# A graph layer kernel: the edge table walked by source block, convolution sums kept in PSUM, and the table zeroed in one stream at the start

## What is computed

```python
# layer 0: five steps of a normalised sum over neighbours
w = dinv[row] * dinv[col]                        # with self loops
for _ in range(5):
    m = segment_sum(w[:, None] * h[row], col)
    h = 0.2 * m + 0.8 * x
x = layernorm(x + h)

# layer 1: gated convolution over the edges
gate = silu(edge_attr @ W1.T + b1) @ W2.T + b2                 # (E, 48)
gate = gate + sum(emb[z[src]] * (emb[z[dst]] @ adaptW.T), -1)  # one number per edge
cw   = where(dist < 6, 0.5 * (cos(pi * dist / 6) + 1), 0)
mj   = node_vec[dst]
agg  = segment_sum(gate * h[dst] * (cw * mj)[:, None], src)
tot  = segment_sum(mj, src)
y    = layernorm_affine(h + agg / clip(tot, 1e-8))
x    = layernorm(x + y)
```

## Time and profile before

| | us |
|---|---|
| three executions timed | 6258.89, 6261.76 (median), 6287.83 |
| profiled execution, its span | 6194.9 |
| index_edges | 105.9 |
| adjacency | 2122.3 |
| propagate | 2249.0 |
| chunks of convolve | 1516.9 |
| busy: PE, DVE, POOL, ACT | 4476.3, 3441.7, 2956.9, 2078.0 |
| slot_table zeroed, SP | 52 DMAs of 1249.5 KB |

### The profile page before, as it was taken

How to read it: one execution, slowest core, us unless ns; L and a number is a source line. 1 busy time by engine, 2 the same in 40 slices (tenths; PEclk the granted TensorE clock), 3 DMA queues, 4 the chain that set the end, 5 groups by cost and what they waited for, 6 DMA issues and landing times. The chain is left out here.

```text
span 6194.9 us, 143286 instructions
## 1 busy us (share of the span) xinstructions
PE 4476.3 (72%) x50445; PEld 3376.9 (55%) x50445; DVE 3441.7 (56%) x8812; ACT 2078.0 (34%) x3637; POOL 2956.9 (48%) x2872
## 2 busy tenths in 40 slices
PE   0477667757776758777777877777758888888885
PEld 0234333333333436556555656565548878787885
DVE  2366666666656553233233323332358888888888
ACT  0133333333333321111111111111126666666664
POOL 1454444544445433433433343334327767676765
PEclk9976777677667577787777877877868888888887
DMA  4222222222222235555555555555401111111111
GB/s 90 63 96 95 95 93 98 90 79 84 95 95 95 85 148 207 182 193 205 201 186 195 214 185 196 206 203 186 172 17 52 42 46 44 44 44 44 44 44 26
DMA packets 292648, 710.09 MB, mean 115 GB/s; under 512 B 203212, under 2 KB 232972, under 8 KB 240894
## 3 DMA queue, kind: packets, MB, share of 16 engines
q1 hardware_dynamic: 226190, 577.45, 27.2%
q10 hardware_dynamic: 7488, 80.35, 3.1%
q0 software_dynamic: 58672, 47.56, 2.7%
HBM read 514.57 MB, written 195.39 MB: 115 GB/s over the span
## 5 line engine op out<-in xcount | busy, mean ns | idle before, releaser
L486 POOL DMA_INDIRECT slot_table<-w_pay,w_slot x1750 | 1802.3, 1030 | 2493.7 <-DVEq L651 1931.0
L927 PE MATMUL pL<-p_parts,p_adj 128*128 128x144 bf16 x12250 | 1093.6, 251 | 498.7 <-issue 440.6
L927 PEld LDWEIGHTS pL<-p_parts,p_adj 128*128 128x128 bf16 x12250 | 950.8, 110 | 644.3 <-issue 607.4
L567 ACT ACTIVATE w_hid<-w_pH,b1c 48x512 f32<-48x512 f32 (+1 forms) x450 | 301.8, 671 | 1927.3 <-DMA cw_table<-cw 976.4
L798 PE MATMUL pA<-ohk,ohb 128*128 128x392 bf16 x2400 | 645.8, 421 | 252.1 <-DVE ohk L769 99.5
L647 DVE COPY w_pay<-w_meta 128x24 f32<-128x24 f32 (+1 forms) x250 | 45.5, 182 | 1363.9 <-PE w_pG L534 1024.0
L534 PE MATMUL w_pG<-w2T,w_hid 49*128 49x48 f32 x3500 | 574.6, 310 | 94.1 <-ACT w_hid L567 56.4
L534 PEld LDWEIGHTS w_pG<-w2T,w_hid 49*128 49x128 f32 x3500 | 515.2, 221 | 224.1 <-issue 205.4
L769 DVE TENSOR_SCALAR ohk<-io_k,k 128x392 bf16<-128x392 f16 x2400 | 621.9, 327 | 7.4 <-issue 7.4
L1300 PE MATMUL cG<-c_cur,c_ohdT 128*128 128x81 bf16 x7350 | 552.0, 212 | 67.4 <-issue 64.4
L1302 PE MATMUL cG<-c_emb,c_ohsT 128*128 128x32 bf16 x7350 | 534.4, 183 | 78.6 <-issue 78.6
(11 more groups left out here) (229 smaller groups left out, 6139.9 us busy)
## 6 DMA issues: line engine op xcount, KB each, us to landing
p_adj<-adj_table SPq DMA_DIRECT2D x250, 1568.0 KB
adj_table<-adj ACTq DMA_DIRECT2D x50, 1568.0 KB
slot_table<-zero SPq DMA_DIRECT2D x52, 1249.5 KB
c_rows<-slot_table SPq DMA_DIRECT2D x50, 1249.5 KB, 5.4
w_attr<-in_edge_attr_dram SPq DMA_DIRECT2D x50, 700.0 KB
slot_table<-w_pay,w_slot POOLq DMA_INDIRECT x1750
kw<-key_table SPq DMA_DIRECT2D x800, 1.5 KB
out_dram<-h_all SPq DMA_DIRECT2D x1, 1152.0 KB
```

What stands on the lines that cost most here:

```text
L486: pool.indirect_dma_start(slotT, bass.IndirectOffsetOnAxis(ap=slot[:, t:t + 1], axis=0), pay[:, t, :], None, bounds_check=SLOTS - 1, oob_i ...
L927: x_ = nc.tensor.matmul(pL[:, half, o * H3:(o + 1) * H3], adj[:, q, n * P:(n + 1) * P], parts[:, n, :, :].rearrange("p t f -> p (t f)"), s ...
```

## The change

The slot table is laid out by source block: a slot's address was (D, r, S) and is now (S, r, D), so `slots_of` takes a source block, `pos` is built from a new per-window tile `home` = S * 128 * 49 + inv, and the base of a destination block grows by 1 instead of 49 * 128. `convolve` walks source blocks outside and destinations inside, 49 x 7 = 343 chunks. All chunks of one source block add into the same 147 columns of PSUM, so the sums stay there for seven chunks, and DVE takes them out once (`take_sums`). One matmul of 147 columns per bucket covers the three parts of its messages. The parts are no longer bf16 tiles: the moving operand is the upper 16-bit half of each fp32 word, read in place with a step of two, and POOL makes the second and third words by two subtractions one after the other (`lower_parts`), without ACT. `tabp` (destination features) is read by PE directly, and the small `cur` holds the source block's embedding. The first body of 14 chunks now stands ahead of the loop, the loop runs 23 times, and seven chunks stand behind it. The clears at the start of `convolve` are gone except that of `c_gx`. The whole slot table (49 regions) is zeroed by ACT at the start of `index_edges`, ahead of Sin on that engine; POOL waits once for all of it before its first scatter; SP no longer zeroes, and `s_clear` is gone.

```diff
-        slots_of = lambda D: slotT.rearrange("(d r s) w -> r d (s w)", r=P, s=NB)[:, bass.ds(D, 1), :]
+        slots_of = lambda S: slotT.rearrange("(s r d) w -> r s (d w)", r=P, d=NB)[:, bass.ds(S, 1), :]
...
             @block.scalar
             def _(act):
+                if beside:
+                    beside(act)
                 act.wait_ge(s_arg, 1)
                 nc.scalar.activation(cw[:, :], cw[:, :], ACT.Sin, bias=halfpi[0:SP_, :], scale=-pi / CUTOFF).then_inc(s_sin, 1)
...
+                    def zero_slots(act):
+                        act.wait_ge(s_z, 1)
+                        for S in range(NB):
+                            act.dma_start(slots_of(S), zero[:, :].unsqueeze(1)).then_inc(s_zero, 16)
+                    cut = cutoff("icut", block, ew, cw, zero_slots)
...
-                        for D in range(2):
-                            sp.dma_start(slots_of(D), zero[:, :].unsqueeze(1)).then_inc(s_zd, 16)
...
-                        sp.wait_ge(s_zd, 16 * 2)
...
+                        nc.vector.memset(zero[:, :], 0.0).then_inc(s_z, 1)
                         nc.vector.memset(bad[:, :], 0.0)
-                        nc.vector.memset(zero[:, :], 0.0).then_inc(s_z, 1)
...
+                nc.vector.scalar_tensor_tensor(home[:, :], f_i[:, 0, :], float(P * NB), inv[:, :], ALU.mult, ALU.add)
...
-                            for n in range(2):
-                                sp.dma_start(slots_of(2 * it + 2 + n), zero[:, :].unsqueeze(1)).then_inc(s_zd, 16)
...
+                        pool.wait_ge(s_zero, 16 * NB)
                         with pool.Fori(0, ND // 2) as it:
-                            pool.wait_ge(s_clear, it + 1)
                             win.scatter(pool, it)
...
+                msg = sb("c_msg", [P, 4, 3, CH * W1c], F32, c)
+                upper = msg[:, :, :, :].rearrange("p q t f -> p (q t f)").bitcast(BF16).rearrange(
+                    "p (q t j w e) -> p q t j w e", q=4, t=3, j=CH, e=2)[:, :, :, :, :, 1]
...
+                        def lower_parts(k, i):
+
+                            q = RING[k % NCK]
+                            pool.wait_ge(s_msg, i + 1)
+                            nc.gpsimd.tensor_tensor(part(k, 1), part(k, 0), upper[:, q, 0, :, :], ALU.subtract).then_inc(s_r1, 1)
+                            pool.wait_ge(s_r1, i + 1)
+                            nc.gpsimd.tensor_tensor(part(k, 2), part(k, 1), upper[:, q, 1, :, :], ALU.subtract).then_inc(s_r2, 1)
...
-                        nc.vector.memset(tabp[:, ND - 1, :, :], 0.0)
-                        nc.vector.memset(agg[:, :, :], 0.0)
-                        nc.vector.memset(gx[:, :, :], 1.0)
...
+                        nc.vector.memset(gx[:, :, :, :], 1.0)
...
-                            nc.vector.tensor_tensor(A, A, pO[:, par, 0:CH * W1c].rearrange("p (s w) -> p s w", w=W1c), ALU.add).then_inc(s_agg, 1)
...
+                            dve.wait_ge(s_O, S * NCK + NCK)
+                            nc.vector.tensor_reduce(agg[:, bass.ds(S, 1), :].rearrange("p o w -> p (o w)"),
+                                                    pO[:, u, 0:W3].rearrange("p (t w) -> p w t", w=W1c), AX, ALU.add).then_inc(s_agg, 1)
...
-                            nc.scalar.activation(mp[:, (k - 1) % 2, 0, :, :], msg[:, (k - 1) % 2, :, :], ACT.Copy).then_inc(s_p0, 1)
...
-                            nc.scalar.activation(mp[:, (k - 1) % 2, 1, :, :], msg[:, (k - 1) % 2, :, :], ACT.Copy).then_inc(s_p1, 1)
...
                             for j in range(CH):
-                                for t in range(3):
-                                    m = nc.tensor.matmul(pO[:, k % 2, j * W1c:(j + 1) * W1c], ohs[:, (k - 2) % NCK, :, j], mp[:, k % 2, t, j, :],
-                                                         start=t == 0, stop=t == 2)
+                                m = nc.tensor.matmul(pO[:, u, 0:W3], ohs[:, ck, :, j], upper[:, RING[ck], :, j, :],
+                                                     start=ck == 0 and j == 0, stop=ck == NCK - 1 and j == CH - 1)
```

184 lines of the change are left out of this document (81 added, 103 removed).

## The result

| | us | ratio to the kernel before |
|---|---|---|
| before, timed beside it | 6272.15 (4 runs) | |
| changed kernel | 6336.81 (6327.26 to 6347.6) | 1.010 [1.007, 1.0131] |
| forecast | 6285, 6195 to 6372 | |

The change made the kernel 1.0% slower, 64.7 us where +23 was forecast.

A forecast was written before the change was run, and what follows sets the result against it. Index_edges was taken as bound by round trips, adjacency by POOL waiting for DVE, convolve by DVE without gaps; +128 - 15 - 90 gave +23 on 6261.8, so 6285 us, range 6195 to 6372.

The forecast's parts named there:

- rival C: Convolve: strided 16-bit reads leave no gain per chunk; convolve -35 us, total 6340; chance 0.18.
- Rival B: Index_edges: ACT's issues aren't held or loads keep their share; +45 to +60 us, total 6212, faster; chance 0.22.
- The stream: Index_edges: zeroing 62.7 million bytes at 398 GB/s lasts 157 us, starting near 25 us.
- Who waits for it: Index_edges: ACT is held by its zeroing issues, Sin runs at about 178 us, and the stage grows by 128 us.
- rival D: Index_edges: `first_i` starved by packet turns, landing at 182 us, Sin at 211; stage +150 us, total 6307; chance 0.20.
- A: The forecast itself, with ACT held in index_edges until some 7 regions are left; own range 6240 to 6330 us; chance 0.40.
- Adjacency: Adjacency without zeroing on SP gains 0.6 us in each of 25 iterations: -15 us, bounds -60 and +25.
- A chunk: Convolve: an undisturbed chunk falls from 3.61 to 3.47 us, the larger of two computed limits; bounds 3.25 and 3.75.
- the round of POOL and DVE: Convolve: POOL and DVE exclude each other, so their operations in turn limit a chunk to 3.47 us.
- the loop through PE: Convolve: the dependency loop through the sums spans two chunks and limits one to 3.40 us, or 3.64 at half speed.
- Convolve in all: Convolve: shorter chunks 48, seven fewer 25, one turn fewer 7, less 5, prologue clears 5: -90 us.
- The base: Whole kernel: the median lies 66.9 us above the profiled span of 6194.9, taken to stay the same around it.

The follow-up runs named there:

- e6: The kernel before, unchanged, profiled on chip 2 in one set with e5b; span 6171.6 us.
- e5b: The changed kernel, unchanged, profiled again on chip 2 in one set with e6; span 6217.6 us.
- e5: The changed kernel, unchanged, run again on chip 3; 4872.37 us, ratio 1.0052 to the kernel before on that chip.
- e8: The changed kernel with ACT starting the zeroing only once `first_i` has landed; index_edges took 221.3 us against 241.9 in the changed kernel on that chip.
- e10: The changed kernel with one of the seven sum matmuls per chunk of convolve; chunks took 1190.5 us together against 1401.3 in the changed kernel.
- e2: The kernel before with only the zeroing moved: all 50 regions by ACT ahead of Sin; 6302.22 us, ratio 1.021 to the kernel before.
- e7: The changed kernel with the old slot numbers and without `home`; adjacency took 1641.9 us against 1631.2 in e5.
- e4b: The changed kernel with the sums reading a contiguous bf16 table, not every second half-word; convolve's chunks took 1397.1 us against 1404.5 in e5.
- e11: The changed kernel with 24 regions zeroed behind Sin, 25 at adjacency's start, and convolve's loop written out; 4623.26 us, ratio 0.9539 to the kernel before.

## Why the prediction was near, step by step

The time fell in the range, 52 us above the predicted 6285, and slower was the likelier side. As a change it is less near: +23 was forecast, and the sets have +64.7 (the first), +46 (the pair e6 and e5b) and +23.1 (e5, chip 3). That the sum of the stages came out close was in part luck. In the pair, index_edges (+8.5) and adjacency (+33) lay above the forecast, propagate, held at 0, took +11.8, and convolve with its prologue lay 29 below. The time is also next to rival C's 6340 and outside the forecast's own 6240 to 6330, but C said that a chunk gains nothing, and it gained 0.225 us. What made the +65 of the first set larger than the +46 of the pair isn't known. Rival B (0.22) fell with index_edges: it had +45 to +60. By the sign that the prediction set itself, no stage held unchanged moved by more than 30 us: propagate with norm0 has +26.8 in the first profiles and +11.8 in the pair.

- **The stream** (step: 157 us at 398 GB/s from 25). Right: the DMA engines moved 408 GB/s from 25.70 to 146.72, and from 180 on ACT's queue moved less than 0.1 MB.
- **Who waits for it** (step: ACT is held, Sin at 178, index_edges +128). The size was near, +136.5, but the mechanism that set it was rival D, to which I gave 0.20: `first_i` at 179.40 (182 worked out), Sin at 207.32 (211). The working of D had one number wrong: SP's queue had moved 9167 packets, most of `first_i`, by 28.8, so that some 430 elements per DMA engine were unread and not 750. That is still as many as the stream had packets per engine (392 rows and the small ones that end each DMA), and so `first_i` came in with the stream's end; with half as many unread it would have come half way through, by the same taking of turns (an estimate from the 935 against 935). D's own sum for the stage was +150: Sin came 4 us sooner than it had it, and what follows Sin was 7 us shorter than before, since the two zeroings are gone from its end. ACT was held as in A, but only to 146.7: at 0.41 MB per us some 39 regions had been written by then, so about ten stood in its queue and not seven. e8 shows that both mechanisms exist one behind the other.
- **Adjacency** (step: -15). The gain isn't there: +18 in the pair, which is within what two like profiles differ by (29, e5b and e10), and e2, with no iteration shorter, shows that nothing was to be won: the zeroing rode beside work with nothing behind it, as the earlier trace rows said. The 0.6 us per iteration had no row. What makes the changed kernel's adjacency longer on the slower chips isn't settled.
- **A chunk** (step: 3.47 from the round of POOL and DVE; the loop through PE 3.40). The loop was right to 0.02 (3.385) and was the binding one. The round was mis-sized: 3.24 (e10) where I added 3.47. e10's chunk from 4926.35 to 4929.60 has, against the terms of my sum: `c_ohd` and `c_gx` 1.30 (1.30), what of `c_ohs` lies behind `c_gx` 0.54 (0.58), what of L1109 lies behind `c_ohs` 0.62 (0.70), the gap 0.08 (0.05), L1111 0.76 (0.79), and `c_ohd` starts 0.05 before L1111 ends (0.05 behind it). No single term was far out; all but the gap were a little too long. S was 0.55 for 0.48: 147 columns and not 144, and 9 ns each for the step; the rest of the loop was 0.10 shorter than worked out.
- **Convolve in all** (step: -90). It was -119 with the prologue (-112.0 - 7.1). Undisturbed chunks gave more, 342 x (3.61 - 3.385) = 77 for my 48. The turn of the loop saved (7) gave nothing: 23 turns cost 174 us before (23 chunks of 257.2 us where 83 are due) and 22 cost 177 in the changed kernel.
- **The base.** I treated the 66.9 us between the profiled span and the median as time around the span. It is 4 to 5 us. The sum was added to the median as a difference, so the forecast didn't suffer; the sum on the span, 6218, would have been 62 us further off.
- **What I passed over.** The 7.48 us at each turn of the loop was in my hands, and I took it as given ("one turn fewer, 7"). It was the largest item in convolve: 22 turns, 177 us. The profile's line for q8, 280 packets in the kernel before, is the row that would have told it.

## What to carry to other kernels

A transfer of many small elements starved here when another queue was given large rows, since the two queues took turns by packets and not by bytes, and everything that waited for it came behind the whole stream: look at what is in flight when a long stream starts, and not only at what its own issuer does next. When a loop's turn shows an idle time that no data explains, look at the instruction queue, and count the instructions of the longest engine's body; writing the loop out can be worth more than the change one set out to make. Compare stages only between profiles from one set of runs, and profile the same kernel twice there before reading a difference of 1%.

## What the runs showed of the hardware

The chips differ, and only in some stages. The changed kernel on chip 3 (e5), propagate with norm0:

```profile
1895.86:3363.97 1468.11, 1375.71 (x15498) 1134.81 (x15498) 768.35 (x1957) 337.34 (x530) 950.74 (x875) 0.96 0.83 300
```

and on chip 2 (e5b):

```profile
2398.73:4713.10 2314.37, 1750.86 (x15498) 1344.44 (x15498) 757.05 (x1957) 338.75 (x530) 865.55 (x875) 0.78 0.54 190
```

Adjacency is 1631.2 us on the one and 2134.2 on the other. Index_edges (241.9 and 241.8) and the chunks of convolve (1404.5 and 1401.3) are the same on both within 0.3%. In propagate TensorE does the same 12250 matmuls at L923 with the same median length of 226 ns, but without a wait that the profile shows ("issue") its weight loads (PEld) stood idle for 43.1 us on chip 3, and on chip 2 its matmuls for 444.8 us and its weight loads for 602.0. The two overlap, so they don't add up to idle time of the engine. First chip 3, then chip 2:

```profile
PEld pL L923 <- issue: 43.1, 29, 7.0
```

```profile
PEld pL L923 <- issue: 602.0, 631, 6.7
PE pL L923 <- issue: 444.8, 552, 1.9
```

The DMA engines moved 300 GB/s there on chip 3 and 190 on chip 2. The granted clock of TensorE was 0.96 and 0.78. Propagate is 1468 us long on the one and 2314 on the other. Whether the gaps, the lower clock or the slower DMA comes first, and what the engine waits for in the gaps, wasn't tried. All experiments but e8, e5, e7, e4b and e11 ran on the slower chips.
